# A small language-model block: value products of the first 24 units with fp32 weights, and a new order of work around the first block

## The reference

```python
h = tok(x)                     # emb_table[x], rms norm, projection 512x512, rms norm
h = h + attn(layernorm(h))     # causal, 32 heads of 16, 8 key/value heads, softmax, output 512x512
h = h + ffn(layernorm(h))      # silu(h @ gate) * (h @ up), 512 -> 2048, @ down, 2048 -> 512
```

## Time and profile before

| | |
|---|---|
| median of 3 runs | 752.84 us (749.26 to 752.88) |
| the profiled execution | 748.56 us |
| its span, first to last instruction | 746.8 us |
| busy: TensorE, its weight loads | 686.7 us (92%), 511.6 us (68%) |
| busy: VectorE, ScalarE, GpSimd | 444.3 us (59%), 358.4 us (48%), 355.2 us (48%) |
| mean granted TensorE clock | 0.977 of full speed |

### The profile page before, as it was taken

The page is one execution under the profiler, slowest core; times in us unless marked ns, Lnnn a source line. Parts: engine busy times, 40 slices in busy tenths (PEclk is TensorE's granted clock), DMA queues, the critical chain, the costliest instruction groups (busy, mean ns, idle before and its releaser), DMA issues.

```text
span 746.8 us, 16350 instructions
## 1 busy us (share of the span) xinstructions
PE 686.7 (92%) x6314; PEld 511.6 (68%) x6314; DVE 444.3 (59%) x1072; ACT 358.4 (48%) x725; POOL 355.2 (48%) x449
## 2 busy tenths in 40 slices
PE   7636878868899999999999999999999999999998
PEld 4434647755489847985699659964897489857873
DVE  6888989889565546645565546563655465444320
ACT  6955656666256513662266316641565146521320
POOL 7024535787237543664266516653465437530220
PEclk9957899999999999999999999999999999999999
DMA  8959020001100011001200120003000210000000
GB/s 323 415 165 352 18 89 3 1 1 40 50 29 2 3 59 59 2 1 46 73 1 3 39 79 2 2 1 103 16 2 2 66 51 2 2 15 15 1 1 29
DMA packets 10461, 40.39 MB, mean 54 GB/s; under 512 B 1808, under 2 KB 2576, under 8 KB 8592
## 3 DMA queue, kind: packets, MB, share of 16 engines
q1 hardware_dynamic: 6912, 25.44, 8.8%
q0 software_dynamic: 3328, 13.11, 5.6%
q10 hardware_dynamic: 144, 0.79, 0.3%
HBM read 29.89 MB, written 9.44 MB: 53 GB/s over the span
## 4 chain that ended last, share of the span: by engine, by line
PE 73%; DVE 13%; POOL 4%; issue 4%; ACT 3%; DMA 3%; SPq 0%; DVEq 0%; POOLq 0%; ACTq 0%
PE banks L1079 12%; PE banks L1081 12%; PE banks L1080 12%; PE banks L1107 6%; PE banks L1109 6%; PE banks L1108 6%; PE banks L995 3%; PE banks L1036 2%; PE banks L1038 2%; PE banks L1037 2%; PE banks L984 2%; DVE gate_work L779 1%; PE banks L1008 1%; DVE ffn_weights L732 1%; PE banks L1009 1%
## 5 line engine op out<-in xcount | busy, mean ns | idle before, releaser
L1079 PE MATMUL banks<-xnT_and_h,ffn_weights 128*128 128x256 f16 x1024 | 279.6, 273 | 3.3 <-DVE ffn_weights L732 3.3
L1081 PE MATMUL banks<-xnT_and_h,ffn_weights 128*128 128x256 f16 x1024 | 279.8, 273 | 0.0
L1080 PE MATMUL banks<-xnT_and_h,ffn_weights 128*128 128x256 f16 x1024 | 279.6, 273 | 0.0
L360 POOL TENSOR_TENSOR gated_split<-gate_work,gated_split 128x256 f16<-128x256 f32 x128 | 86.5, 676 | 238.2 <-ACT gated_split L495 238.0
L364 POOL TENSOR_TENSOR weights_split<-weights,weights_split 128x512 f16<-128x512 f32 x128 | 153.3, 1199 | 19.5 <-ACT weights_split L501 19.5
L1079 PEld LDWEIGHTS banks<-xnT_and_h,ffn_weights 128*128 128x128 f16 x1024 | 100.2, 98 | 15.2 <-issue 3.7
L485 ACT ACTIVATE gate_work<-banks,scales 128x256 f32<-128x256 f32 x128 | 60.4, 472 | 100.6 <-PE banks L1081 100.6
L1081 PEld LDWEIGHTS banks<-xnT_and_h,ffn_weights 128*128 128x128 f16 x1024 | 100.3, 98 | 11.9
L1080 PEld LDWEIGHTS banks<-xnT_and_h,ffn_weights 128*128 128x128 f16 x1024 | 100.3, 98 | 11.5
L491 ACT ACTIVATE weights<-banks,scales 128x512 f32<-128x512 f32 x128 | 87.1, 681 | 36.5 <-PE banks L995 36.4
L757 DVE COPY q_stack<-banks 128x256 f16<-128x256 f16 x128 | 36.8, 288 | 106.3 <-PE banks L984 106.1
(11 more groups left out here) (228 smaller groups left out, 1065.2 us busy)
## 6 DMA issues: line engine op xcount, KB each, us to landing
ffn_weights<-in_ffn_w SPq DMA_DIRECT2D x12, 1024.0 KB, 14.9
out_rows_dram<-ffn_weights SPq DMA_DIRECT2D x16, 256.0 KB, 2.0
xnT_and_h<-in_wqkv SPq DMA_DIRECT2D x1, 1536.0 KB, 8.4
local_table<-gated_split SPq DMA_DIRECT2D x2, 640.0 KB, 5.9
local_table<-xnT_and_h SPq DMA_DIRECT2D x2, 640.0 KB, 3.6
gated_split<-in_projT SPq DMA_DIRECT2D x4, 256.0 KB, 4.3
ffn_weights<-in_wo SPq DMA_DIRECT2D x1, 1024.0 KB, 10.4
token_table<-weights_split ACTq DMA_DIRECT2D x1, 768.0 KB, 8.7
```

Source lines behind the costliest of these rows:

```text
L360: g.tensor_tensor(gtl[:, j, :], g2[j % 2], gth[:, j, :], ALU.subtract).then_inc(gt_lo, 1)
L1079: t.matmul(o, wh, xTh[m % 2][:, c, :], start=c == 0, stop=False)
L1080: t.matmul(o, wh, xTl[m % 2][:, c, :], start=False, stop=False)
L1081: last = t.matmul(o, wl, xTh[m % 2][:, c, :], start=False, stop=c == DC - 1)
```

## The change

- Units 0 to 23 (`WIDE`) keep their weights in fp32: `values` uses the fp32 weights as the stationary operand and v in fp32 with a one (`v_full_one`, 17 columns) as the moving one, 4 matmuls a unit in the program, two slots after the unit's score instead of three. The cast on ScalarE and the subtraction on GpSimd fall away for them. `v_full_one` is the sum of v's two halves, one GpSimd instruction.
- In block 0, pairs of units alternate between two PSUM banks, and VectorE reads numerator and denominator from PSUM and writes y; no copy by ScalarE, nothing on GpSimd.
- In blocks 0 and 1 the stack copies are made by ScalarE; from block 2 on by VectorE, as before.
- All weight halves in `split_high` are made by ScalarE.
- The slots of block 0's end, of the group steps, of the Gram matmuls, of the weight scales and of the fills are new: no fills before slot 20. Statistics of the two tiles get their own columns.
- Gate-up chunk 0 stands ahead of turn and score of unit 16.

```diff
-POOL_HALVES = (6, 8, 10, 12, 14)
+VFW = HD + 1
+WIDE = UPB + 8
 
 EPS_RMS, EPS_LN = 1e-6, 1e-5
 NEG = -3.0e38
@@ -45,21 +46,19 @@
 SEEN_MAX = 1.5
 TINY = 1e-30
 
-FIRST_SLOTS = dict(yt=(13, 20), wo=(15, 21), ln=(16, 21), xhat=(16, 21), xn=(19, 22), fetch=(20, 22), m=(23, 3))
+FIRST_SLOTS = dict(yt=(11, 18), wo=(13, 19), ln=(16, 20), xhat=(17, 20), xn=(19, 21), fetch=(17, 20), m=(21, 3))
 SECOND_SLOTS = dict(yt=(15, 20), wo=(16, 21), ln=(17, 21), xhat=(17, 21), xn=(19, 23), fetch=(18, 22), m=(22, 3))
 LATER_SLOTS = dict(yt=(13, 20), wo=(14, 21), ln=(15, 21), xhat=(16, 21), xn=(18, 23), fetch=(18, 22), m=(22, 3))
 HI_FIRST = {16: 0, 17: 1, 20: 2, 21: 3, 22: 4}
-LOW_FIRST = {20: (0, 1), 21: (2,), 23: (3,)}
+LOW_FIRST = {18: (0,), 20: (1,), 21: (2,), 23: (3,)}
 HI_NEXT = {-1: 4, 0: 5, 1: 6, 3: 7, 4: 8, 6: 9, 7: 10, 8: 11, 9: 12, 11: 13, 12: 14, 13: 15, 14: 16, 15: 17, 16: 18, 17: 19, 18: 20,
            19: 21, 20: 22, 21: 23}
-FILL = {**{s: 2 for s in range(17)}, 17: 4, 18: 4, 19: 4, 20: 4, 21: 6, 22: 6}
+FILL = {20: 6, 21: 6, 22: 4}
 SECOND_MAX_SLOT = 4
-Y_ON_POOL = 17
-Y_ON_DVE = (Y_ON_POOL - 5) // 2
-GROUP_SLOTS = range(4, 12)
-GRAM = {s: (6 * (s - 6), min(64, 6 * (s - 5))) for s in range(6, 17)}
-DN_BOUND_SLOT, DN_SUM_SLOT, DN_MAX_SLOT, DN_SCALE_SLOT = 19, 21, 23, 3
-GU_SCALE_SLOT = 2
+GROUP_SLOTS = range(0, 8)
+GRAM = {16: (0, 8), 17: (8, 16), 18: (16, 32), 19: (32, 48), 20: (48, 64)}
+DN_BOUND_SLOT, DN_SUM_SLOT, DN_MAX_SLOT, DN_SCALE_SLOT = 21, 22, 23, 3
+GU_SCALE_SLOT = 8
...
+        def pv_bank(pair):
+            return f_bank[1] if pair < UPB // 2 and pair % 2 == 1 else b_PV
+
+        def lag(V):
+            return 2 if V < WIDE else 3
+
+        def ev_slot(pair):
+            return 2 * (pair % (UPB // 2)) + 1 + lag(2 * pair)
...
+            pool.wait_ge(tab["vl"], 1)
+            g.tensor_tensor(Vf3[:, :, 0:HD], Va3[:, :, 0:HD], Va3[:, :, HD:2 * HD], ALU.add).then_inc(tab["vf"], 1)
...
+                    if att and 1 <= s <= UPB and n * UPB + s - 1 >= WIDE:
                         V = n * UPB + s - 1
-                        pool.wait_ge(wt_hi, V + 1)
+                        pool.wait_ge(wt_hi, V + 1 - WIDE)
...
+                        num = pv[:, :, HD:2 * HD]
+                        if 8 * t + 2 * i >= WIDE:
+                            g.tensor_tensor(yv, pv[:, :, 0:HD], num, ALU.add).then_inc(num_rdy, 1)
+                            pool.wait_ge(num_rdy, 4 * t + i + 1 - WIDE // 2)
+                            num = yv
                         pool.wait_ge(rd_rdy, 4 * t + i + 1)
-                        last = g.tensor_tensor(yv, yv, rden[k][:, 8 * i:8 * i + 8].unsqueeze(2).broadcast_to([P, 8, HD]), ALU.mult)
+                        last = g.tensor_tensor(yv, num, rden[k][:, 8 * i:8 * i + 8].unsqueeze(2).broadcast_to([P, 8, HD]), ALU.mult)
...
-                        if HI_NEXT.get(s) in POOL_HALVES:
-                            split_high(HI_NEXT[s])
...
-                last = a.activation(half(i, 0)[:, 0:512], raw(i)[:, 0:512], ACT.Copy, scale=s_g if i < 16 else s_d)
-                if i not in POOL_HALVES:
-                    last = a.activation(half(i, 0)[:, 512:1024], raw(i)[:, 512:1024], ACT.Copy, scale=s_u if i < 16 else s_d)
-                last.then_inc(split_hi, 1)
+                a.activation(half(i, 0)[:, 0:512], raw(i)[:, 0:512], ACT.Copy, scale=s_g if i < 16 else s_d)
+                a.activation(half(i, 0)[:, 512:1024], raw(i)[:, 512:1024], ACT.Copy,
+                             scale=s_u if i < 16 else s_d).then_inc(split_hi, 1)
+
+            def stack(V):
+                actq.wait_ge(q_tr, V + 1)
+                if V >= RING:
+                    actq.wait_ge(scores, V - RING + 1)
+                r = V % RING
+                a.activation(Qst[:, r * 256:(r + 1) * 256], b_Q[:, 0:256], ACT.Copy).then_inc(q_st, 1)
 
             def phase(n, att, ffn, m):
                 at = (FIRST_SLOTS, SECOND_SLOTS, LATER_SLOTS)[min(n, 2)]
                 for s in range(SLOTS):
+                    if n == 1 and s == 0:
+                        split_high(HI_NEXT[0])
+                        stack(UPB)
+                    if att and n <= 1 and s + 1 < UPB:
+                        stack(n * UPB + s + 1)
...
+                        if V >= WIDE + RING:
+                            actq.wait_ge(wt_lo, V - RING + 1 - WIDE)
+                        elif V >= RING:
+                            actq.wait_ge(pv_rdy, V - RING + 1)
...
+                    if n == 0 and 3 <= s < UPB + 3 and s % 2 == 1:
+                        k, i = divmod((s - 3) // 2, 4)
+                        pair = 4 * k + i
+                        dve.wait_ge(pv_rdy, 2 * pair + 2)
+                        pv = pv_bank(pair)[:, 0:2 * REP * VFW].rearrange("p (h c) -> p h c", c=VFW)
+                        v.reciprocal(rden[k][:, 8 * i:8 * i + 8], pv[:, :, HD]).then_inc(rd_rdy, 1)
+                        dve.wait_ge(rd_rdy, pair + 1)
+                        yv = y[k][:, i * P:(i + 1) * P].rearrange("p (h d) -> p h d", d=HD)
+                        v.tensor_tensor(yv, pv[:, :, 0:HD], rden[k][:, 8 * i:8 * i + 8].unsqueeze(2).broadcast_to([P, 8, HD]),
+                                        ALU.mult).then_inc(pv_ev, 1)
+                        if i == 3:
+                            dve.wait_ge(pv_ev, pair + 1)
+                            v.tensor_scalar(st[:, 25:26], rden[k][:, 0:1], 1.0, None, ALU.mult).then_inc(y_rdy, 1)
...
+                if V < WIDE:
+                    pe.wait_ge(w_rdy, V + 1)
+                    if V == 0:
+                        pe.wait_ge(tab["vf"], 1)
+                    for h in range(REP):
+                        o = pv_bank(V // 2)[:, ((V % 2) * REP + h) * VFW:((V % 2) * REP + h + 1) * VFW]
+                        last = t.matmul(o, E[r][:, h * P:(h + 1) * P], Vf3[:, gr, :], start=True, stop=True)
+                    last.then_inc(pv_rdy, 1)
+                    return
...
+                    if ffn and m == 0 and s == 0:
+                        gate_up(0, 0)
+                        turn(UPB)
...
+                    for u in range(UPB):
+                        if att and s == u + lag(n * UPB + u):
+                            values(n * UPB + u)
...
+                    if ffn and s < HC and (m > 0 or s > 0):
+                        gate_up(m, s)
```

More of the change, by code:

```diff
@@ L97, in lm_block @@
         Va3 = Va[:, :].rearrange("p (g c) -> p g c", g=KV)
+        Vf = sb("v_full_one", KV * VFW, F32)
+        Vf3 = Vf[:, :].rearrange("p (g c) -> p g c", g=KV)
         ident = sb("ident", P, F32)
@@ L343, in _ @@
             fetch_rows(1)
[L345 to L351, removed]
             def phase(n, att, ffn, m):
@@ L495, in phase @@
                         a.activation(gth[:, j, :], g2[j % 2], ACT.Copy).then_inc(gt_hi, 1)
-                    if att and 1 <= s <= UPB:
+                    if att and 1 <= s <= UPB and n * UPB + s - 1 >= WIDE:
                         V = n * UPB + s - 1
@@ L501, in phase @@
                         a.activation(WTh[V % RING], E[V % RING][:, :], ACT.Copy).then_inc(wt_hi, 1)
-                    if att and 4 <= s < UPB + 4 and s % 2 == 0:
-                        i = (s - 4) // 2
+                    for i in range(UPB // 2):
+                        if not (att and n > 0 and s == ev_slot(n * UPB // 2 + i)):
+                            continue
                         k, gp = divmod(i, 4)
@@ L533, in phase @@
                             split_high(HI_FIRST[s])
-                    if n == 1 and s in HI_NEXT:
+                    if n == 1 and s > 0 and s in HI_NEXT:
                         split_high(HI_NEXT[s])
+            stack(0)
             phase(0, True, False, 0)
@@ L772, in phase @@
                         store_rows(n * TPB - 3)
-                    if att and s + 1 < UPB:
+                    if att and n > 1 and s + 1 < UPB:
                         stack(n * UPB + s + 1)
@@ L801, in phase @@
                                      .rearrange("p (h c) -> p h c", c=PVW)[:, :, 2 * HD]).then_inc(rd_rdy, 1)
[L802 to L810 removed]
                     for k in range(TPB):
                         t = n * TPB + k
+                        ln = st[:, 26 + 12 * k:38 + 12 * k]
                         if att and s == at["yt"][k]:
@@ L843, in phase @@
                         store_rows(m * TPB)
-                    if att and s == 23 and n + 1 < BLOCKS:
+                    if att and n > 0 and s == 23 and n + 1 < BLOCKS:
                         stack((n + 1) * UPB)
@@ L864, in _ @@
             place_max(0)
-            stack(0)
             phase(0, True, False, 0)
@@ L1010, in values, with gate_up @@
                 last.then_inc(pv_rdy, 1)
+            def gate_up(m, s):
+                i = m * HC + s
+                if s == 0:
+                    pe.wait_ge(xt_lo, m * TPB + TPB)
+                    if m > 0:
+                        pe.wait_ge(g2_rdy, i)
+                if s == 2 and m == 0:
+                    pe.wait_ge(tab["dn_max"], 1)
```

(14 more changed lines are left out.)

80 lines of the change are left out of this document (23 added, 57 removed).

## The result

The changed kernel takes 748.66 us (median of 12 runs, 747.06 to 750.15), the kernel before, run beside it, 752.94 (12 runs, 748.61 to 754.17). The ratio is 0.9961, 95% interval 0.9944 to 0.9977: 4.3 us faster by the medians, where I had forecast 9.5 and a time of 743.

A forecast was written before the change was run, and what follows sets the result against it. TensorE was taken to bound the kernel from the third block on, leaving blocks 0 and 1 to change: 748.6 - 1.8 - 7.7 = 739.1 us profiled, 743 as median; 8 in 10 for 733 to 751.

The forecast's parts named there:

- Block 0's attention: Block 0's unit loop through the last value product: fp32 products at half clock, +1.7 us, bounds -9 and +12.
- Block 0's tail: Block 0 from last value product to gate-up chunk 0: shorter by 3.5 us, bounds -2 and -4.5.
- Chunk 0 is issued ahead of turn, stack and score: End of block 0: chunk 0 no longer waits behind unit 16's transposes, stack and score, -1.8 us.
- y's last pair: End of block 0: y goes from PSUM to VectorE, no longer through ScalarE and GpSimd, -1.7 us with two waits.
- Block 1, slots 0 to 8: First nine slots of block 1: TensorE sets them with fp32 products, 3.83 us a slot, 33.4 us together.
- Block 1, slots 9 to 14: Rest of block 1's first 15 slots: fp16 path and VectorE's loss return, 23.0 us together.
- rival 3: Block 1: ScalarE's order delays VectorE's gate, slots stay at 4.2 us, gain 1 us or less; 750 us, chance 0.17.
- The base: Whole kernel: the median was put 4.3 us above the profile's 739.1, giving 743.3.
- Both signs: Prediction wrong if ScalarE ends block 1's waits, or stages behind 174 us change by more than 1 us.
- The splits of slots 0 to 8: Block 1, expected in the profile after: VectorE's weight splits near 0.75 us each.
- Rival 1: Block 0: clock rises to 2.4 GHz or half-clock pitch is 0.11, slot 1.25 to 1.5 us; 735 us, chance 0.24.
- Rival 2: Cold fp32 loads follow at 0.312 us, block 0's 13 units cost 10.6 us more; 756 us, chance 0.09.

The follow-up runs named there:

- second profile: The kernel before, unedited, profiled once more to look into its two groups of run times: 751.34 us (one run).

## Why the prediction was wrong

By its own steps, profile against profile, in us: forecast, then measured. The first four steps below, the set-up (+0.7), the down slots (+1.4) and the later blocks (-0.5) make up, rounded, the 0.9 between the profiles.

- *Block 0's attention* +1.7, measured +1.1 (from the first transpose to the last product, 41.4 before, 42.4 after). Right, and for the reason given: half clock until 89.5, TensorE sets a slot of 2.34 (measured 2.27), pitch 0.21. Exp of unit 0 to that of unit 15 took 36.0 (forecast 37.6), from there to the last product 4.4 (forecast 4). wo of tile 0 took 5 us and not 4: in the timeline its matmuls follow by 0.43 from 85.0 to 89.2, the clock rising only at 89.5.
- *Block 0's tail* -3.5, measured +0.8. **This step failed.** "Chunk 0 is issued ahead of turn, stack and score" (-1.8) took for granted that nothing else stands between xn and chunk 0 in TensorE's program. The sum matmul does, behind a VectorE step that the change put two slots later. From the operand being ready (109.02) to chunk 0 (112.41) it took 3.4 us instead of none; moving the step gave 2.7 of it back at chunk 0, the rest is the fills. The other term, -1.7 for y's last pair, came to -0.8: from the last product to the operand 13.2, 14.0 before. TensorE was at 1.2 GHz from 92.9 to 99.7 there and at 2.4 from 88.2 on before, which may be what is missing; no run separates it. The step also counted "today's" transposes and stack ahead of chunk 0 as pure gain. Chunk 0 to chunk 1 is 4.7 us, forecast 3.6, and 4.6 with the transposes ahead, so the stack copies behind the splits on ScalarE cost as well.
- *Block 1, slots 0 to 8* -2.2 (33.4), measured -0.4, 35.2 for the nine: 1.1 of the 1.8 missing stand in slot 0 (4.7 instead of 3.6), the other 0.9 in slot 1. I had given slot 1 2.95, without an fp32 value product; but product 16 stands between chunks 1 and 2 in TensorE's program, so the slot took 3.82 like the seven behind it (forecast 3.83). TensorE sets them, as forecast.
- *Block 1, slots 9 to 14* 23.0 (-5.4), measured 26.3 (-2.1). **This failed too.** I took one VectorE slot, 4.1 (slot 13 of the kernel before), for the pace from slot 12 on. Slots 9 to 11 took 9.3 (10.8 forecast), then 7.1, 4.8 and 5.1. Slot 12 alone is 3.1 us over its 4.05, and before's own trace had it at 7.1: split, tanh, gate, split and chunk follow each other there, one slot ahead of the chunk, and the change left that chain as it was. Behind TensorE's wait came a half-clock spell (164.6 to 168.0), and slot 13 took 4.8, 3.2 in the run with a split in every slot, where no spell came. Slot 14 is rival 3's mechanism: the stack copy waits for TensorE's transposes and holds back tanh, and tanh VectorE's gate.

```profile
168.85 0.38 ACT L484 ACTIVATE q_stack<-banks 128x256 f16<-128x256 f16 x1 [1.98 <-PE banks L1009]
...
169.64 0.42 DVE L801 SCALAR_TENSOR_TENSOR gate_work<-gate_work,banks 128x256 f32<-128x256 f32 x1 [1.65 <-ACT gate_work L500]
```

  With the copies on VectorE the slot took 4.5. That the splits could have been done in the shade of slots 1 to 8 was shown: 23.0 us for the same stretch. That this is the forecast's number is luck, for its slots were 3.2 to 4.05 and the measured ones lie between 2.95 and 5.54.
- *The base.* I added 4.3 us to the sum because the median stood 4.3 above before's profile. The changed kernel's median stands 0.8 *below* its own profile. Before's runs spread over 5.6 us, the changed kernel's over 3.1, at a clock of 0.952 to 0.961. That offset belonged to the old kernel. The sum missed the profile by 10.4 us (739.1 against 749.5) and the offset missed by 5.1 the other way, so the median was missed by 5.4 alone.

Both signs that the prediction gave for being wrong were there. VectorE's gate waited 7.4 us in all for ScalarE's tanh in block 1 (3.3 before), and the stage behind 174 us was 1.4 longer, which the second profile of the kernel before shows too. The splits of slots 0 to 8 were forecast near 0.75 each. Their second halves took 0.78 on average, their first halves 1.13, with GpSimd's one subtraction a slot (0.67) beside them.

Rival 1 (the loop goes to full clock by itself) did not come, though TensorE was busy without a gap (last section). The rule of the Trainium skill cited there ("TensorE: Matmul & The Clock Gate", "What's actually happening"), that the clock follows how busy TensorE has been, disagrees with this trace if weight loads are taken for busy time. What rival 1 would have met was described rightly: with the clock raised, tile 0's yT waited 4.88 us for the group table. Rival 2 (0.312 pitch) is refuted by the pitch of 0.21. The load time without a clock beside it in the Trainium skill ("TensorE: Matmul & The Clock Gate", "LDWEIGHTS (loading the stationary operand)"), 107 ns, disagrees with it too: the trace shows that pitch at full clock only.

Open: why the kernel before has two groups of times. The second profile is longer by 1.0 us in block 0 and 1.3 in the down slots, out of some 4 between the groups, and the slower executions have the lower granted clock; what decides where the half-clock spells fall is not shown.

## What to carry to other kernels

When work on an engine that runs in program order is moved ahead of something, list every instruction that is left between it and what it waits for, above all small side jobs with a semaphore from another queue: one such matmul cost more here (2.7 us) than the reordering was to bring (1.8). When several engines build something in a ring, one step ahead of its use, move it into the shade of the slots that another engine bounds; here that was worth 6.9 us, more than the whole change. Before taking one slot of the old trace for the pace of a stretch, list all of its slots: the one of 7.1 us stood there. And a fill that nobody reads may carry the clock of the real work: before taking it out, look at the granted clock of that stretch and at what else will stream there.

## What the runs showed of the hardware

TensorE stayed at 1.2 GHz for 41 us (48.5 to 89.5). From the first value product on it was busy without a gap, mostly with fp32 products of 17 columns, which follow each other at the pitch of their weight loads:

```profile
57.48:89.50 32.02, 32.02 (x179) 29.05 (x178) 15.01 (x46) 12.15 (x25) 0.00 (x0) 0.50 0.53 201
```

With the same loads and instructions and a moving operand of 112 columns it rose to 2.4 GHz at 62.9 us, and the columns cost little: the 8 matmuls of a unit in 2.00 us instead of 1.83 at half clock, in 1.10 instead of 1.02 at full, 3.89 instead of 3.82 for a slot of block 1. That makes widening a moving operand behind fp32 loads nearly free here. The pitch of the fp32 products follows the clock, 0.21 and 0.11 us, while fp16 products of 33 columns follow by 0.025 at full clock.
